# Issuing the output store two slots earlier on SyncE in a hand-scheduled transformer layer

## The reference

```
# attention: 16 heads of 16 features, 4 groups of keys and values
qkv = x @ Wqkv + bqkv                       # (16, 256, 384)
q, k, v = split(qkv); k, v tiled over the heads of their group
prob = softmax(q k^T / 16);  out = prob v
x1 = layernorm(x + out @ Wout + bout)
# feed-forward, 1024 wide, weights rounded to three values per group of 64
gate, up = split(x1 @ ternary(w_gate_up)^T)
h = silu(gate) * up;  hn = rms_norm(h)
y = layernorm(x1 + hn @ ternary(w_proj)^T)
```

## Time and profile before

| | us |
|---|---|
| median of 3 executions | 596.38 |
| lowest, highest | 593.19, 597.74 |
| the profiled execution, its own time | 593.19 |
| its span, first to last instruction | 591.4 |
| mean granted clock of TensorE, as a share of 2.4 GHz | 0.984 |

### The profile page before, as it was taken

The page is one execution under the profiler, slowest core; times in us unless marked ns, Lnnn a source line. Parts: engine busy times, 40 slices in busy tenths (PEclk is TensorE's granted clock), DMA queues, the critical chain, the costliest instruction groups (busy, mean ns, idle before and its releaser), DMA issues.

```text
span 591.4 us, 14163 instructions
## 1 busy us (share of the span) xinstructions
PE 551.1 (93%) x4368; PEld 465.8 (79%) x4368; DVE 441.8 (75%) x1033; ACT 370.1 (63%) x738; POOL 330.7 (56%) x437
## 2 busy tenths in 40 slices
PE   6669999999999999999999999999999999898983
PEld 5668777788888888888888888888888888786873
DVE  7875766777787868787778778787878787866675
ACT  5454935566666666757567666667576666567552
POOL 5575761253655656564745565465657375565773
PEclk9798999999999999999999999999999999999998
DMA  6955365444351717153544526170725354010001
GB/s 227 154 137 72 81 94 99 74 100 74 81 110 56 134 38 118 39 115 77 103 86 86 102 67 121 45 140 16 134 43 117 72 99 92 1 38 18 3 18 37
DMA packets 53932, 49.08 MB, mean 83 GB/s; under 512 B 6144, under 2 KB 53888, under 8 KB 53888
## 3 DMA queue, kind: packets, MB, share of 16 engines
q1 hardware_dynamic: 51152, 47.60, 40.1%
q10 hardware_dynamic: 2736, 0.92, 0.7%
HBM read 33.29 MB, written 14.68 MB: 81 GB/s over the span
## 4 chain that ended last, share of the span: by engine, by line
PE 72%; DVE 14%; DMA 4%; issue 3%; SPq 2%; POOL 2%; ACT 1%; ACTq 1%; DVEq 0%; POOLq 0%
PE ffn_ps L545 17%; PE short_ps L470 11%; PE pv_ps L573 10%; PE short_ps L517 8%; PE down_ps L558 8%; PE exp_ps L526 8%; PE short_ps L581 6%; DVE st L935 2%; DVE r L932 2%; DVE row_max L807 2%; DVE gated L855 2%; DVE h_f L862 1%; ACTq L777 1%; DMA xn<-in_L_attn_x_dram 1%; DMA k_dram<-k_p 1%
## 5 line engine op out<-in xcount | busy, mean ns | idle before, releaser
L807 DVE TENSOR_REDUCE row_max<-short_ps 128x2 f32<-128x512 f32 x256 | 173.7, 681 | 54.8 <-PE short_ps L517 54.8
L976 POOL TENSOR_TENSOR h_lo<-h_f,h_hi 128x256 fp32r<-128x256 f32 x128 | 94.8, 740 | 189.1 <-ACT h_hi L703 177.9
L721 ACT ACTIVATE probs<-exp_ps 128x1024 f32<-128x1024 f32 x128 | 130.9, 1023 | 29.0 <-PE exp_ps L526 25.6
L517 PE MATMUL short_ps<-k_st,q_st 65*128 65x256 f32 x512 | 116.7, 310 | 12.1 <-DVE row_max L807 7.6
L712 ACT ACTIVATE tanh<-ffn_ps 128x256 f32<-128x256 f32 x120 | 45.8, 382 | 110.6 <-PE ffn_ps L545 93.6
L517 PEld LDWEIGHTS short_ps<-k_st,q_st 65*128 65x128 f32 x512 | 82.4, 193 | 22.4 <-issue 7.8
L545 PE MATMUL ffn_ps<-x1T_hi,wguT 128*128 128x256 f32 x480 | 81.6, 293 | 7.1 <-DVE h_f L862 7.0
L526 PE MATMUL exp_ps<-q_st,k_st 67*128 67x512 f32 x256 | 81.5, 400 | 0.7 <-DMA q_st<-shift_lo 0.6
L981 POOL TENSOR_TENSOR sq_sum<-sq_sum,h_sq 128x256 f32<-128x256 f32 x105 | 77.9, 742 | 0.0
L558 PE MATMUL down_ps<-wpT,h_hi 128*128 128x256 f32 x256 | 75.6, 317 | 2.2 <-POOL h_lo L976 2.2
L545 PE MATMUL ffn_ps<-x1T_lo,wguT 128*128 128x256 f32 x480 | 77.3, 283 | 0.0
(11 more groups left out here) (102 smaller groups left out, 889.4 us busy)
## 6 DMA issues: line engine op xcount, KB each, us to landing
q_st<-q_dram SPq DMA_DIRECT2D x128, 128.0 KB, 4.1
q_dram<-q_p SPq DMA_DIRECT2D x16, 512.0 KB, 3.0
xn<-in_L_attn_x_dram SPq DMA_DIRECT2D x16, 256.0 KB, 4.2
k_st<-k_dram SPq DMA_DIRECT2D x64, 64.0 KB, 2.2
res<-in_L_attn_x_dram SPq DMA_DIRECT2D x16, 256.0 KB, 4.5
out_dram<-y_out SPq DMA_DIRECT2D x16, 256.0 KB, 4.1
wgu_raw<-in_L_ffn_w_gate_up_dram SPq DMA_DIRECT2D x8, 256.0 KB, 6.5
k_dram<-k_p SPq DMA_DIRECT2D x16, 128.0 KB, 3.1
```

Source lines behind the costliest of these rows:

```text
L517: last = pe.matmul(bank[:, t * S:(t + 1) * S], q_st[0:PAD, st.par, head, t * P:(t + 1) * P], k_st[0:PAD, st.par, st.s % 4, :], start=True, ...
L721: act.activation(probs[:, st.s % 4], exp_ps[:], ACT.Exp).then_inc(exp_done, 1)
L807: dve.tensor_reduce(row_max[:, st.par, head * TT:(head + 1) * TT], short(n, f"max{i}")[:].rearrange("p (t k) -> p t k", t=TT), AX.X, ALU.m ...
L976: pool.tensor_tensor(h_p[1][:, st.s % 4, :], h_f[:, st.s % 2, :], h_p[0][:, st.s % 4, :].bitcast(F32), ALU.subtract).then_inc(h_lo, 1)
```

## The change

The offset of the store goes from 47 to 45. So SyncE waits for `y_done` and issues the store in phase 5, after STACK_QK of phase 3 and ahead of LOAD_RES and STACK_REST of phase 7. LAST becomes two slots smaller; no step of any engine stands in those two.

```diff
 LN2_STATS = 42
 LN2_APPLY = 45
-STORE = 47
+STORE = 45
```

## The result

The changed kernel takes 613.94 us (median of 5, 613.76 to 618.09) against 596.38 (5 runs, 593.19 to 597.8): slower, ratio 1.0322, 95% interval 1.0273 to 1.0371. That is 17.6 us more, where 10 were forecast. The profiled execution took 615.71 us, with a span of 613.9 (22.5 more than the span before) and a mean granted clock of 0.966 instead of 0.984. The profiled execution of before, 593.19, was the fastest of its five and this one lies above its median, so the pair of profiles shows more than the 17.6 us between the medians.

The account below looks back on a forecast made before the run. PE's in-order matmul list was taken as the bound. Its new waits for xn, 7.8 + 0.4 + 2.1 = 10.3, say 10 us, on 596.4 gave 606.5 us, range 598 to 616.

Parts of the forecast that it names:

- PE's own list is the bound, and its waits are paid in full: Steady stretch: PE busy 321.5 of 325.0 us, 32.0 us a batch, with almost no idle time to catch up.
- y_done replaces the exp scores as the gate, with nine transfers between it and LOAD_X: SyncE's queue: LOAD_RES and eight stack transfers wait for y_out's end, 1.2 us after the old gate.
- The path from y_out's end to the first k_st, 1.6 in the loop, 1.0 written out: SyncE's queue: release, store address, store, LOAD_RES and gaps; first k_st 2.7 us later than before in the loop.
- From the first k_st to xn landed, 8.4: SyncE's transfers ahead of xn set its landing: 8.4 us as in batch 5, upper end 10.0.
- The waits, 10.3 in sum: PE waiting for xn: 1.3 us in six loop batches, 0.4 in batch 10, 0.7 each in batches 6 to 8.
- A batch grows by its wait: PE's loop batches: about 1.3 us idle on xn each, the batch going from 32.0 to 33.3 us.
- What costs nothing: Earlier store unneeded; later transfers keep cover: keys 3 us, residual 7 (8 at the end), second query half 16.
- Rival A: xn lands 3.5 us after its own issue, without backlog: 2.2 us lost, about 598.5 us; chance 0.22.
- Rival B: Residual ahead of the keys adds in full, 10.0 us to xn's landing: 26 us lost, 622; chance 0.09 including half way.
- Rival C: Kernel gets faster, which would need some wait of PE to get shorter; chance 0.03.

Follow-up runs that it names:

- The wait alone: Kernel before the change, with only the wait for y_done put into phase 5 and the store left in phase 7: 608.26 us, ratio 1.0243.
- the same list with y_done sooner: Changed kernel with y_out made one slot earlier (LN2_APPLY 45 to 44), SyncE's order unchanged: 594.07 us, ratio 0.998.
- filler: Changed kernel with eight, then four identity matmuls on PE ahead of the wait for xn in batches 6 to 15: 613.56 us, then 611.01 us.

## Why the prediction was right, and where it was off

- *PE's own list is the bound, and its waits are paid in full*: right. The batches at full clock grew by 1.5 us where the recorded wait is 1.34 on average.
- *y_done replaces the exp scores as the gate, with nine transfers between it and LOAD_X*: right. The wait alone (1.0243) and the same list with y_done sooner (0.998) show it; and taking one transfer out from behind it (1.0135), or four (0.9989), shows that what stands there counts by the piece.
- *The path from y_out's end to the first k_st, 1.6 in the loop, 1.0 written out*: 1.5 to 1.8 in six of the seven, 2.0 in batch 9, and 1.0 (168.83 to 169.81 in batch 6). The 0.2 for setting the store's address, for which the prediction had no row, came out: the store goes 0.25 to 0.28 after y_out's end in the loop. LOAD_X left 1.9 to 2.2 later against y_out in eight batches, 1.3 in batch 9 and 2.9 in batch 8, where 1.7 to 2.1 was forecast.
- *From the first k_st to xn landed, 8.4*: this term was too small, above all where it mattered most. It measures 7.9 to 8.9 in the loop, 8.58 on average, and 9.1, 9.1 and 9.3 in batches 6 to 8 (169.81 to 173.64 + 5.3 in batch 6). I took it from batch 5, where no residual stands ahead of the keys, and argued that the engines would be empty for it; they were not quite. The run with the residual out of the way gives 8.45 in the loop and 8.66 in batches 6 to 8, so the residual's bytes make some 0.1 and 0.5 of it. The truth lies between batch 5's row and batch 3's 10.0.
- *The waits, 10.3 in sum*: 13.4. Of the 3.1 us that are missing, batches 6 to 8 make 1.8 (1.3 each and not 0.7, by the path above), batch 10 makes 0.7 and the other six 0.6. In batch 10 the sum counted on PE being late by itself; that was 0.9 us of waits for h_f in the profile of before, which did not come again in the profile after (0.3).
- *A batch grows by its wait*: it grew by 1.5 where the wait is 1.34, so the ten batches grew by some 15.
- *The sum had no term for the clock.* It took the 1.00 of the earlier trace rows as given. The waits are just what takes it away: four drops cost 5.8 us in the profiled execution. Between the two profiles the 22.5 us are thus 15 of delay, 5.8 of clock and 1.7 outside the ten batches. How the 17.6 us between the medians divide is not known, since they have no profile.
- *What costs nothing*: right in all points. In the ten batches no engine waited for keys, residual or second half of the queries, in any run.
- Rival A, no backlog, fell: a load lands 3.9 to 5.3 after its issue, and the path that it wanted under 7.4 is 7.9 at the least. No load of xn in these batches landed sooner than 3.3 after its issue in any run, so the shorter time that would have made its price nothing was never seen. Rival B in full fell too, though a part of its mechanism, the residual's bytes, is in the 0.1 and 0.5 us above. Rival C: no run was faster.
- The batch was forecast at 33.3 us; it was 33.6, or 35.1 with a clock drop.
- That 613.94 lies under the range's upper end of 616 is partly luck. That end stood for half of rival B with the noise of the runs, the residual's bytes at 0.8 a batch. Of these the runs show 0.1 to 0.6, some 2 us in all. What filled the rest was batch 10, the growth of a batch beyond its wait and the clock, for none of which the range had a term.

## What to carry to other kernels

Before moving a wait in an in-order queue, list what is queued behind it and how much slack each has; here the one with 1.3 us decided, and the engine that issued it was nearly idle. If a wait must move, look for transfers behind it that can change places: the same early store costs nothing when the queries that are wanted last go behind the load that is wanted first. And price a stall of TensorE in a busy stretch with more than its length: some of them are followed by microseconds of half clock.

## What the runs showed of the hardware

- Waits of PE of 1.2 to 1.9 us in the ten batches were followed by the half clock 13 times: the granted clock fell to 0.50 in the last 0.6 us of the wait or within 1.4 us after it, for some 3 us (in two cases for twice that). In the batches with one such fall of some 3 us PE was busy 1.5 us longer. It happened four, two and four times in the three profiles of the changed kernel, once where only the wait was moved, twice with xn from ScalarE's queue, and never in the run with eight waits of 1.1 us and less, with filler, or where PE did not wait for xn. Fifteen other waits of 1.2 to 2.1 us passed without a fall. What decides was not settled.
- In the loop the store leaves 0.25 to 0.28 us after the end of the y_out that releases it; there the kernel works out its address in registers. Where slots are written out it leaves after 0.03 (y_out's end 168.83, store 168.85).
- A store of 256 KB that leaves some 7 us behind SyncE's last transfers lands 2.2 us after its issue in the median; before the change, directly behind the stack, it took 4.1.
